# An fp32 input projection written as three float32r matmuls per block, with split operands

## The reference

```
h = layernorm(x) * (1 + ca) + sa
xc, z = split(h @ W_in)              # W_in is 128 x 512
xs = silu(causal conv of xc, 4 taps)
...                                  # selective scan over time
x = x + ga * ((y + D * xs) * silu(z)) @ W_out
h = layernorm(x) * (1 + cb) + sb
x = x + gb * (shared FFN(h) + top-2 of 8 expert FFNs(h))
```

## Time and profile before

| | |
|---|---|
| median of 3 runs | 744.22 us |
| the profiled execution | 742.37 us |
| its span, first to last instruction | 740.6 us |
| mean granted TensorE clock | 0.94 of full |
| VectorE busy | 550.7 us (74%) |
| ScalarE busy | 440.0 us (59%) |
| GpSimd busy | 397.0 us (54%) |
| all 64 PE records of `hT` by `w_in` | 34.0 us |

### The profile page before, as it was taken

One profiled execution on the slowest core, in us unless ns is written; L12 is line 12 of the kernel. 1 busy time (PEld: TensorE's weight loads), 2 busy tenths in 40 slices (PEclk: granted clock), 3 DMA queues, 4 the chain that ended last, 5 costly groups with the idle time before them and its releaser, 6 DMA issues.

```text
span 740.6 us, 12188 instructions
## 1 busy us (share of the span) xinstructions
PE 651.5 (88%) x3026; PEld 501.9 (68%) x3026; DVE 550.7 (74%) x1220; ACT 440.0 (59%) x804; POOL 397.0 (54%) x329
## 2 busy tenths in 40 slices
PE   4778989889998989878778999999999999999960
PEld 1555766667675667656556877877878878777840
DVE  5787988989798997987565776677776667666752
ACT  4647666685767668563444666666666666666640
POOL 2424564738456464826245847567439448472560
PEclk9688989999899999998889999999999999999995
DMA  8303111202112020211331324241320414211407
GB/s 260 78 1 102 50 50 37 64 28 75 39 57 57 29 57 28 82 32 65 108 129 44 114 78 150 66 145 52 122 72 30 157 40 122 99 49 65 135 30 232
DMA packets 47381, 59.83 MB, mean 81 GB/s; under 512 B 8756, under 2 KB 34856, under 8 KB 47360
## 3 DMA queue, kind: packets, MB, share of 16 engines
q1 hardware_dynamic: 41600, 46.91, 20.9%
q0 software_dynamic: 5760, 12.67, 4.9%
HBM read 40.01 MB, written 20.84 MB: 82 GB/s over the span
## 4 chain that ended last, share of the span: by engine, by line
PE 51%; DVE 30%; issue 10%; ACT 2%; DMA 2%; POOL 2%; DVEq 1%; SPq 1%; POOLq 0%; ACTq 0%
PE PS L671 48%; PE PS L674 4%; DVE al L1322 4%; DVE acc L1335 3%; DVE prod L1315 2%; DVE dB L1359 2%; DVE yT L1425 1%; DVE wd L1408 1%; DVE PS L1315 1%; DVE h L1447 1%; DMA yT<-result_dram 1%; DVE stats_a L1299 1%; DVE diag L1412 1%; DVE stats_b L1299 1%; DVE nx_b L1434 1%
## 5 line engine op out<-in xcount | busy, mean ns | idle before, releaser
L1034 ACT ACTIVATE sg<-PS 128x512 f32<-128x512 f32 x216 | 128.7, 597 | 131.9 <-PE PS L671 121.7
L671 PE MATMUL PS<-xh,w_lo 128*128 128x512 f32 x405 | 176.1, 435 | 13.2 <-DVE prod L1315 10.4
L1315 DVE TENSOR_TENSOR PS<-PS,sg 128x512 f32<-128x512 f32 (+1 forms) x160 | 111.3, 697 | 91.7 <-PE PS L671 60.6
L671 PE MATMUL PS<-xl,w_hi 128*128 128x512 f32 x405 | 163.8, 404 | 0.0
L671 PE MATMUL PS<-xh,w_hi 128*128 128x512 f32 x405 | 163.4, 404 | 0.0
L547 POOL DMA_INDIRECT sorted_dram<-h,slot x64 | 73.4, 1147 | 93.0 <-DVE slot L1524 66.9
L671 PEld LDWEIGHTS PS<-xh,w_lo 128*128 128x128 f32 x405 | 78.4, 194 | 46.1 <-DVE prod L1315 16.4
L609 POOL DMA_INDIRECT result_dram<-y_rows,aux_d x84 | 83.0, 989 | 37.5 <-issue 20.1
L1042 ACT CAST ah<-PS 128x512 fp32r<-128x512 f32 (+1 forms) x160 | 93.0, 581 | 15.4 <-DVE PS L1315 13.3
L671 PE MATMUL PS<-ah,w_lo 128*128 128x512 f32 x216 | 93.7, 434 | 8.1 <-ACT ah L1042 4.3
L1322 DVE TENSOR_TENSOR al<-PS,ah 128x512 fp32r<-128x512 f32 x140 | 95.7, 684 | 3.4
(11 more groups left out here) (199 smaller groups left out, 1153.1 us busy)
## 6 DMA issues: line engine op xcount, KB each, us to landing
xin<-sorted_dram SPq DMA_DIRECT2D x20, 516.0 KB
stage<-in_w_gu SPq DMA_DIRECT2D x18, 448.0 KB
sorted_dram<-pad SPq DMA_DIRECT2D x9, 516.0 KB
h<-mods_dram SPq DMA_DIRECT2D x32, 128.0 KB, 6.2
stage<-in_w_dn SPq DMA_DIRECT2D x9, 448.0 KB
tab<-mods_dram SPq DMA_DIRECT2D x8, 384.0 KB, 3.4
out<-X SPq DMA_DIRECT2D x8, 256.0 KB, 5.1
stage<-result_dram SPq DMA_DIRECT2D x6, 256.0 KB, 4.2
```

Source lines behind the costliest of these rows:

```text
L671: return nc.tensor.matmul(out, lhsT, rhs, start=start, stop=stop, **k)
L1034: A.activation(dst, src, ACT.Silu).then_inc(s["silu_done"], 1)
L1315: V.tensor_tensor(product_in(where, c)[0:n, :], bank("up", where, c)[0:n, :], sg[0:n, c % 3, :], ALU.mult).then_inc(s["prod_done"], 1)
```

## The change

- `w_in` is split once into `w_in_hi` (float32r) and `w_in_lo` by GpSimd, `split_w_in`: a multiplication by ones and a subtraction, each over 128x512. TensorE waits for both ahead of the first `turn_x`.
- `modulate` writes `hT` as before and then copies it to `hT_hi` in float32r (ScalarE). GpSimd subtracts, `hT_lo` = `hT` - `hT_hi` (`low_head`): for group 0 behind the split of `w_in`, for group g+1 in body g between `pairs_by_b` and `split_piece`.
- `project_in` issues three float32r matmuls instead of one in float32: low weight by high data, high by high, high by low. Its first block waits for `hT_hi`, and ahead of its third matmul for `hT_lo`.
- In the expert part `xin` becomes a view of `xcp`, `y_rows` is `diag` and `gw` is `nx_b`. Two memsets of VectorE in the start go.

```diff
--- before.py
+++ after.py
@@ -164,6 +164,10 @@
         shift_n = sb("shift_n", [P, CH])
         nx_a = sb("nx_a", [P, GC, P])
         hT = sb("hT", [P, GT])
+        hT_hi = sb("hT_hi", [P, GT], F32R)
+        hT_lo = sb("hT_lo", [P, GT], F32R)
+        w_in_hi = sb("w_in_hi", [P, 4, P], F32R)
+        w_in_lo = sb("w_in_lo", [P, 4, P], F32R)
         xcp = sb("xcp", [P, 2, GS, SEQ + TAPS - 1])
         acc = sb("acc", [P, 2, GT])
         xsT = sb("xsT", [P, 2, GT])
@@ -225,11 +229,10 @@
         al = sb("al", [P, 3, TILE], F32R)
         y_sb = sb("y_sb", [P, TILE])
         gated = sb("gated", [P, TILE])
-        xin = sb("xin", [P, TR, ROW])
-        y_rows = sb("y_rows", [P, TR, P])
+        xin = xcp[:].rearrange("p h q t -> p (h q t)")[:, 0:TR * ROW].rearrange("p (r d) -> p r d", r=TR)
+        y_rows, gw = diag, nx_b
         aux_next = sb("aux_next", [P, TR, P + 2])
         aux_prev = sb("aux_prev", [P, TR])
-        gw = sb("gw", [P, TR, P])
         aux_d = sb("aux_d", [P, TR], I32)
 
         half = [v[:].rearrange("p h t -> p (h t)")[:, k * GT:(k + 1) * GT] for v in (acc, xsT, sz, xs_tok) for k in range(2)]
@@ -267,7 +270,7 @@
 
         names = """passed first_in consts_in x_in x_more c_in setup_mem stage_clear silu_c mods_pe mods_cols mods_rows mods_out a_neg_ready
             tab_in tab_free tab_g_in tab_g_free
-            var_a eps_a rstd_a shift_a nx_ready nxT_done hT_ready xz_done tap_ready conv_done sz_ready xs_ready
+            var_a eps_a rstd_a shift_a nx_ready nxT_done hT_ready hT_hi[:]gh hT_lo[:]w w_in_split xz_done tap_ready conv_done sz_ready xs_ready
             dbc_done dbc_ready xst_done xst_ready nabs_ready exp1_done soft_ready delta_ready cexp_ready spans_done
             cg_done levels_in pairs_in levels_exp pairs_exp pq_ready pqT_done pqT_ready cg_used pairs_ready
             m_done mT_ready mo_ready y_done y_ready o_done var_b eps_b rstd_b shift_b nx_b h2_ready h2_both h2T_done
@@ -491,6 +494,21 @@
                 V.tensor_tensor(w_lo[1][:, at], stage[:, at], w_hi[1][:, at].bitcast(F32), ALU.subtract).then_inc(
                     s["piece_done"], 1)
 
+            def split_w_in():
+
+                flat = "p m t -> p (m t)"
+                pool.wait_ge(s["first_in"], 16 * NFIRST)
+                V.tensor_tensor(w_in_hi[:].rearrange(flat), w_in[:].rearrange(flat),
+                                M["ones"][:, 0:1].to_broadcast([P, 4 * P]), ALU.mult).then_inc(s["w_in_split"], 1)
+                pool.wait_ge(s["w_in_split"], 1)
+                V.tensor_tensor(w_in_lo[:].rearrange(flat), w_in[:].rearrange(flat),
+                                w_in_hi[:].bitcast(F32).rearrange(flat), ALU.subtract).then_inc(s["w_in_split"], 1)
+
+            def low_head(g):
+
+                pool.wait_ge(s["hT_hi[:]gh"], g + 1)
+                V.tensor_tensor(hT_lo[:], hT[:], hT_hi[:].bitcast(F32), ALU.subtract).then_inc(s["hT_lo[:]w"], 1)
+
             def low(I, c):
 
                 pool.wait_ge(s["ah_ready"], I * FC + c + 1)
@@ -565,6 +583,8 @@
             V.memset(pad[:, :, P + 1:P + 2], float(NOWHERE)).then_inc(s["setup_mem"], 1)
             pool.wait_ge(s["setup_mem"], 2)
             head_root(1, 0, GC)
+            split_w_in()
+            low_head(0)
 
             pool.wait_ge(s["consts_in"], 16 * NCONST)
             expand_c(0)
@@ -572,6 +592,8 @@
 
             def body(g, prev, head):
                 pairs_by_b(g)
+                if head:
+                    low_head(g + 1)
                 if not prev:
                     head_root(3, GC + EARLY, LATE)
                     head_root(4, GC + EARLY + LATE, CH - GC - EARLY - LATE)
@@ -753,10 +775,15 @@
                 if m == 1 and tailed:
                     pe.wait_ge(s["counts_read"], g - 1)
                 if m == 0:
-                    pe.wait_ge(s["hT_ready"], g + 1)
+                    pe.wait_ge(s["hT_hi[:]gh"], g + 1)
                 elif m > 1:
                     pe.wait_ge(s["tap_ready"], 2 * g + 4 - m)
-                mm(PS[:, X_BANK[m], :], w_in[:, m, :], hT[:]).then_inc(s["xz_done"], 1)
+                out = PS[:, X_BANK[m], :]
+                mm(out, w_in_lo[:, m, :], hT_hi[:], True, False)
+                mm(out, w_in_hi[:, m, :], hT_hi[:], False, False)
+                if m == 0:
+                    pe.wait_ge(s["hT_lo[:]w"], g + 1)
+                mm(out, w_in_hi[:, m, :], hT_lo[:], False, True).then_inc(s["xz_done"], 1)
 
 
             def project_x(g):
@@ -868,6 +895,7 @@
             mm(PS[:, 2, SEQS:2 * SEQS], stage[:, P:2 * P], sc_t[:])
             mm(PS[0:SEQS, 6, :], sc_t[:], stage[:, 2 * P:6 * P]).then_inc(s["mods_pe"], 1)
             pe.wait_ge(s["first_in"], 16 * NFIRST)
+            pe.wait_ge(s["w_in_split"], 2)
             turn_x(0, True, False)
             for m in range(4):
                 project_in(0, m, False)
@@ -1053,6 +1081,8 @@
                                         ACT.Identity, bias=shift_a[:, bass.ds(g * GS + q, 1)],
                                         scale=scale_a[:, bass.ds(g * GS + q, 1)])
                 last.then_inc(s["hT_ready"], 1)
+                act.wait_ge(s["hT_ready"], g + 1)
+                A.copy(hT_hi[:], hT[:]).then_inc(s["hT_hi[:]gh"], 1)
 
             def last_tap(g, h):
 
@@ -1561,8 +1591,6 @@
             V.tensor_copy(base[:], S["region"])
             link(V.tensor_copy(gate_hi[:], gate_w[:]))
             link(V.tensor_tensor(gate_lo[:], gate_w[:], gate_hi[:].bitcast(F32), ALU.subtract))
-            V.memset(gw[:], 0.0)
-            V.memset(y_rows[:], 0.0)
             V.memset(aux_d[:], NOWHERE)
             V.memset(aux_next[:], float(NOWHERE)).then_inc(s["gates_ready"], 1)
             dve.wait_ge(s["setup_mem"], 2)
```

## The result

The change makes the kernel slower. Its median is 755.19 us (six runs, 754.3 to 759.94) against 744.2 for the kernel before on the same chip (six runs, 743.5 to 744.67): ratio 1.0155, 95% interval 1.0132 to 1.0178. The forecast was 753.5, between 747.0 and 758.0. The number was good, but in part by luck: the mechanism was right, its size came out too small, and a stretch that the forecast did not consider gave almost the same amount back.

A forecast was written before the change was run, and what follows sets the result against it. The prediction took VectorE as the bound where the loop's projection lies, TensorE only behind 184.5 us. Start +3.6, first-body matmuls -0.2 and loop +5.9 gave +9.3 us: 744.2 + 9.3 = 753.5, range 747.0 to 758.0.

The forecast's parts named there:

- Start, +3.6: Start: transposes wait for the `w_in` split (+2.5 us), `hT` split and matmuls delay the tap copy (+1.2), memsets dropped (-0.1).
- The -0.1 for the dropped memsets: Start: dropping two memsets ends the 0.16 us gap before the first convolution, -0.1 us.
- First body, "Cost 0; uncovered 0.3": First body: GpSimd's subtraction makes `weigh` some 0.3 us later, covered by VectorE's moments; cost 0, or 0.3 if uncovered.
- part 3: Loop: GpSimd's extra subtraction makes VectorE instructions with both inputs in SBUF stand until GpSimd's is over; +5.9 us.
- The matmuls in the first body, -0.2: First body: one cheaper projection lies on the chain, -0.2 us, with 0 and -0.7 as ends.
- The matmuls in the loop, 0: Loop: up to 0.25 us freed per block goes into TensorE's waits for VectorE (0.69 and 0.97 us); gain 0.
- The loop, +5.9: Six loop iterations: `ex` stands until the pushed-back `w_lo` ends, +0.8 and +1.15 us, three times each; ends 0 and 8.0.
- The upper end of the term, 8.0: Loop: 8.0 us if GpSimd's `w_lo` also has to wait out `diag`, 0.35 us more in each iteration.
- ScalarE's copy, 0: Loop: ScalarE's 0.62 us copy per iteration is covered; cost 0, or 0.6 x 3 = 1.8 us if uncovered.
- the sharing of buffers: Expert part: sharing buffers moves no instruction, since their earlier users are through long before; cost 0.
- "More waits": Rival, 15%: GpSimd waits out `diag` (+2.1), ScalarE's copy uncovered (+1.8), lower TensorE clock more often; together +3 to +5, 757 us.
- the three signs: Wrong if VectorE's small steps keep 0.19 us, `diag`s stay 43.2 us apart, or TensorE's wait for `ranks` shrinks.

The follow-up runs named there:

- no_sub: Changed kernel without GpSimd's `hT_lo` subtraction for all groups but the first, whose low part the third matmul reuses; 746.65 us, ratio 1.0048 to the kernel before.
- no_split: Changed kernel without GpSimd's `hT_lo` subtraction and ScalarE's copy into `hT_hi` for all groups but the first; 747.37 us, ratio 1.0055 to the kernel before.
- turn_early: Changed kernel with TensorE waiting for the split of `w_in` behind the first transposes, not ahead of them; 752.30 us, ratio 1.0122 to the kernel before.
- twice: Changed kernel with GpSimd's `hT_lo` subtraction issued twice from group 2 on, first into an unread buffer; 760.47 us, ratio 1.0237 to the kernel before.
- split_late: Changed kernel with `split_piece` moved from behind `hT_lo` to late in the body, between two FFN subtractions; 748.14 us, ratio 1.0076 to the kernel before.
- late_use: Changed kernel with groups 0 and 1 projected in plain float32 and `split_piece` moved late in the body; 741.68 us, ratio 0.9990 to the kernel before.
- before_late: Kernel before the change with only `split_piece` moved late in the body, between two FFN subtractions; 740.11 us, ratio 0.9959.
- again: The changed kernel, unedited, measured and profiled once more; 754.08 us, ratio 1.0155 to the kernel before.

## Why the prediction was right, and where not

- **Start, +3.6.** Right in size at the end of the kernel: no_sub leaves 3.6 (2.2 to 4.9), no_split 4.1 (2.9 to 5.4). The wait for the split was 2.45 (2.50 forecast). The second half, forecast at 1.2 on top of 1.27, came out as 2.94 against 2.22, both at half pace. The 1.27 of the earlier trace rows was one execution's luck, so one trace carried a term that changes by almost a microsecond between executions of the same kernel. The -0.1 for the dropped memsets did not come: the tap ends at 17.28 + 0.79 = 18.07 and the convolution starts at 18.23, the same gap of 0.16 without them.
- **First body, "Cost 0; uncovered 0.3".** Wrong, by up to 0.95. The step that failed is the choice in part 3 of what can be held: an instruction "with both inputs in SBUF stands". That was too narrow: `away_a`, a TENSOR_SCALAR with one SBUF input, stood for `hT_lo` as well. The Trainium skill (SBUF — State Buffer, Who interferes with whom) lists `tensor_scalar` among the operations that can take the shared pair, and the trace agrees (0.17 us without the subtraction, 1.12 beside it).
- **The matmuls in the first body, -0.2.** Nothing of it can be seen: body 0 takes 34.7 to 34.9 us in no_sub and no_split, and 34.1 and 34.5 in the kernel before. The change's own 38.37 and 36.15 have a long stretch at the lower clock (mean 0.65 and 0.72 where before has 0.84 and 0.80), while turn_early, twice and split_late, with the same subtraction in it, stay below 35. I count that to the executions, though the change has it in two out of two and that isn't shown.
- **The matmuls in the loop, 0.** Right, and shown by no_split and by late_use beside before_late. In the loop VectorE is the bound where the projection lies. A block frees 0.16 us, where up to 0.25 were forecast.
- **The loop, +5.9.** The mechanism was right: `hT_lo` begins 0.08 us behind `hT_hi`, `w_hi` and `w_lo` move back, `ex` stands (1.05 us instead of 0.19), the iterations are longer, and leaving the subtraction out takes all of the standing away. The size was low: again has 8.8 us more than the first execution of before and 8.4 more than the second, and the change's first execution 10.2. The forecast let `ex` wait for the end of `w_lo` but gave `w_lo` its old 1.29 us. It takes 0.22 more in each iteration, because it waits for `diag` in turn, 1.3 in six; 5.9 + 1.3 = 7.2, beside 7.3 of standing measured (5.2 of `ex`, 2.1 of `diag`). The 1.1 us left go with the granted clock, which has a lower part in all six iterations, where the second execution of before has one in four of them. The forecast put that term at nothing in its sum. The upper end of the term, 8.0, was nearer, but in part by luck, with 0.35 us for each wait of `w_lo` and nothing for the clock. GpSimd waiting in turn, which no row had shown, is shown now.
- **ScalarE's copy, 0.** Right (no_split beside no_sub). So was the sharing of buffers: the expert part takes 366.9 to 369.3 us where it took 367.8 to 368.7.
- **"More waits"** was made a rival of 15% and holds in part: GpSimd waits for `diag` (1.3 us in all, 2.1 forecast), and the lower clock comes in each iteration.
- **Body 7, not mentioned.** It gave back 2.5 us. The forecast ended its path at TensorE's waits in the loop and asked nothing of the clock behind it. The measured terms (3.6 + 1 + 8.6) add up to 13 us above the kernel before, which is 757, near the upper end of the range (758.0); this gift brought the result back to within 1.7 us of the forecast. That is luck.

None of the three signs by which the forecast was to be wrong came: `ex` did not keep its 0.19 us, the `diag`s are 44.2 us apart, and the wait for `ranks` grew from 0.69 to 1.17 us.

## What to carry to other kernels

An instruction on an engine with time to spare is priced by what it pushes its successors onto, so list what runs on the other engine at the moments to which each of them moves, small steps included: 1.29 us of GpSimd cost 1.2 us of VectorE's standing per iteration here, and none of it once two neighbours were moved. A saving on TensorE is worth nothing in a stretch where it waits for VectorE, however many times it is made. And before a term rests on one stretch of one trace, compare the spacing of its matmuls with that of another execution: the start differed by 0.95 us between two executions of one kernel, and the granted clock read 1.00 in both.

## What the runs showed of the hardware

- GpSimd and VectorE hold each other up, in whichever order they come. `ex` 0.19 to 1.05 us behind `w_lo`; `w_lo` 1.29 to 1.51 behind `diag`; `w_hi` 1.04 to 1.49 behind `h`. VectorE's `ex` waits to the end of GpSimd's instruction; GpSimd's instructions lose 0.14 or 0.15 us less than the overlap.
- A TENSOR_SCALAR of 128x7 with one SBUF input is held as well (0.17 to 1.12 us).
- A reduction is not held: in iteration 3 of the change `wd`, a TENSOR_REDUCE of 128x1024, runs from 168.55 for 1.21 us while `hT_lo` runs from 168.82 for 1.29, and both are as long as alone (1.21 or 1.22 and 1.27 to 1.29).
- A loop whose iterations are all alike alternates between two lengths (42.2 us at a granted clock of 1.00, 43.2 at 0.92; strictly so in one execution of before, in the other only from the third iteration on). With 1.29 us more work on GpSimd ahead of `split_piece` no iteration is granted 1.00 throughout.
- The granted clock in the profile can read 1.00 where matmuls run at half pace: in the start of the change 128x512 float32r matmuls start 0.42 us apart beside 1.00, and 0.23 apart in the loop.
